# Output projection of the first ten token tiles, moved from its own stage into the last heads of attention

## The reference

```python
def _L0_attn_ref(x, w_qkv, w_out):
    ...
    scores = jnp.einsum('bihd,bjhd->bhij', q, k) * scale
    weights = jax.nn.softmax(scores, axis=-1)
    attn = jnp.einsum('bhij,bjhd->bhid', weights, v)
    concat = attn.transpose(0, 2, 1, 3).reshape(b, t, NUM_HEADS * DIM_HEAD)
    return jnp.einsum('btf,ef->bte', concat, w_out)
...
x = x + 0.5 * _L0_ffn_ref(_layernorm(x, axis=-1), ...)
x = x + _L0_attn_ref(_layernorm(x, axis=-1), L0_attn_w_qkv, L0_attn_w_out)
x = x + 0.5 * _L0_ffn_ref(_layernorm(x, axis=-1), ...)
```

## Time and profile before

| | |
|---|---|
| median of the runs | 4123.88 us |
| the profiled execution, its own time | 4123.62 us |
| its span, first to last instruction | 4121.8 us |
| PE busy | 4007.0 us (97%) |
| DVE busy | 3718.5 us (90%) |
| ACT busy | 2452.9 us (60%) |
| POOL busy | 1097.2 us (27%) |

### The profile page before, as it was taken

How to read it: one execution, slowest core, us unless ns; L and a number is a source line. 1 busy time by engine, 2 the same in 40 slices (tenths; PEclk the granted TensorE clock), 3 DMA queues, 4 the chain that set the end, 5 groups by cost and what they waited for, 6 DMA issues and landing times. The chain is left out here.

```text
span 4121.8 us, 108893 instructions
## 1 busy us (share of the span) xinstructions
PE 4007.0 (97%) x46275; PEld 2419.0 (59%) x46275; DVE 3718.5 (90%) x6367; ACT 2452.9 (60%) x2774; POOL 1097.2 (27%) x1156
## 2 busy tenths in 40 slices
PE   3999999999999999999999999999999999899999
PEld 2777765558864447884454444444444444677777
DVE  7999993689999999999999999999999996799998
ACT  1222225467777777777777777777777778122222
POOL 3888873300000000000000000000000000288886
PEclk8999999999999999999999999999999999999999
DMA  3000002311010110001001001001100100100000
GB/s 134 1 1 1 1 1 100 123 57 29 21 40 20 30 31 28 22 26 35 23 27 32 29 20 40 21 29 31 29 21 28 33 26 9 34 16 16 16 16 21
DMA packets 77710, 125.58 MB, mean 30 GB/s; under 512 B 27688, under 2 KB 56744, under 8 KB 75432
## 3 DMA queue, kind: packets, MB, share of 16 engines
q1 hardware_dynamic: 77224, 118.62, 9.8%
HBM read 72.55 MB, written 36.31 MB: 26 GB/s over the span
## 5 line engine op out<-in xcount | busy, mean ns | idle before, releaser
L1090 DVE TENSOR_REDUCE stats<-ps_b 128x1 f32<-128x512 f32 x4016 | 2486.5, 681 | 106.9 <-PE ps_b L1139 6.3
L1077 ACT ACTIVATE probs<-ps_s 128x1024 f32<-128x1024 f32 x2048 | 1983.8, 1021 | 648.6 <-PE ps_s L1173 648.6
L1139 PE MATMUL ps_b<-w_ffn 96*32 96x512 bf16 x10688 | 1122.5, 381 | 6.2 <-PEq L758 5.9
L1151 PE MATMUL ps_o<-probs,w_qkvT 128*32 128x512 f32 x8192 | 1097.2, 592 | 0.6 <-ACT probs L1077 0.6
L1173 PE MATMUL ps_s<-w_ffn 99*32 99x512 bf16 x10752 | 987.4, 380 | 0.5 <-ACT probs L1077 0.5
L639 PE MATMUL ps_gu_f<-w_ffn,zT_f 128*128 128x352 f32 x2048 | 638.7, 466 | 20.6 <-DVE h_f L514 15.9
L1173 PEld LDWEIGHTS ps_s<-w_ffn 99*32 99x32 bf16 x10752 | 392.0, 98 | 347.1 <-issue 188.4
L1139 PEld LDWEIGHTS ps_b<-w_ffn 96*32 96x32 bf16 x10688 | 379.1, 96 | 350.7 <-issue 174.2
L1139 PE MATMUL ps_b<-K,Q 96*32 96x512 bf16 x5376 | 568.7, 381 | 0.2
L1173 PE MATMUL ps_s<-Q,K 99*32 99x512 bf16 x5632 | 512.2, 381 | 2.2 <-ACT probs L1077 1.8
L639 PEld LDWEIGHTS ps_gu_f<-w_ffn,zT_f 128*128 128x128 f32 x2048 | 384.8, 193 | 217.5 <-issue 20.6
(11 more groups left out here) (150 smaller groups left out, 3460.4 us busy)
## 6 DMA issues: line engine op xcount, KB each, us to landing
w_ffn<-qk_parts_dram SPq DMA_DIRECT2D x84, 192.0 KB
w_ffn<-qk_parts_dram SPq DMA_DIRECT2D x84, 128.0 KB
x_res<-in_L_attn_x SPq DMA_DIRECT2D x4, 2048.0 KB, 19.5
qk_parts_dram<-first_group SPq DMA_DIRECT2D x32, 256.0 KB, 3.0
qk_parts_dram<-factor SPq DMA_DIRECT2D x32, 256.0 KB, 2.9
qk_parts_dram<-qk_parts SPq DMA_DIRECT2D x32, 256.0 KB, 2.8
factor<-denom_dram SPq DMA_DIRECT2D x64, 128.0 KB, 5.3
out<-x_res SPq DMA_DIRECT2D x16, 512.0 KB, 2.7
```

What stands on the lines that cost most here:

```text
L1077: nc.scalar.activation(probs[:, (2 * kt + half) % 4, :], ps_s[:, half, :], ACT.Exp, scale=float(DH) ** -0.5).then_inc(exped, 1)
L1090: nc.vector.tensor_reduce(mx[:, s, k // 4, bass.ds(k % 4, 1)], ps_b[:, bank, :], AX.X, ALU.max).then_inc(bank_free, 1)
L1139: last = nc.tensor.matmul(ps_b[j:j + STRIP, bank, :], Q[s][0:PAIRS, qt * P + j:qt * P + j + STRIP], K[s][0:PAIRS, kb * 512:(kb + 1) * 512] ...
L1151: last = nc.tensor.matmul(ps_o[32 * c:32 * c + 32, :], V[s][:, kt, :], probs[:, (2 * kt + c // 2) % 4, (c % 2) * 512:(c % 2 + 1) * 512], s ...
```

## The change

The first five groups of the output projection (ten tiles of batch 0, whose heads were finished long before) move into attention. `part_of` deals out their 20 products, one for each of the 20 key tiles without maxima: four at the end of head 62 and 16 in head 63. PE issues a product behind the first half's scores of its key tile and ahead of the second half's. The results go to the three banks `ps_b`; behind every fourth product DVE adds the group and takes its statistics. The loops of the last block start at group 5 on PE and DVE. Banks, waits and steps of the groups that stay keep their numbers. The norm's scratch moves from a tensor of its own to free columns of `y`.

```diff
@@ attend_phase, DVE
+                        at = merge.part_of(g, kt)
+                        if at and at[1] == merge.PARTS - 1:
+                            merge.add(dve, merge_bank(at[0]), at[0])
@@ attend_phase, PE
+                def merge_part(i, part):
+
+                    if i == 0 and part == 0:
+                        pe.wait_ge(bank_free, fills_before(NH - 1))
+                        pe.wait_ge(m.out_scaled, 4 * KD * (B - 1))
+                    if i >= RING and part == 0:
+                        pe.wait_ge(merge.x_done, i - RING + 1)
+                    last = merge.multiply(merge_bank(i), i, part)
+                    if part == merge.PARTS - 1:
+                        last.then_inc(merge.y_done, 1)
...
                             if c % 2:
                                 last.then_inc(scored, 1)
+                            at = merge.part_of(g, kt)
+                            if at and c == 1:
+                                merge_part(*at)
@@ Merge
+    EARLY = 5
+    PARTS = G * KD
+    SPARE = 4
...
+    def part_of(self, g, kt):
+
+        at = (g - (B * H - 2)) * KT + kt - (KT - self.SPARE)
+        return divmod(at, self.PARTS) if 0 <= at < self.EARLY * self.PARTS else None
...
-        for i in range(self.NG):
-            b = i // self.PER_BATCH
+        for i in range(self.EARLY, self.NG):
...
-        for i in range(self.NG):
-            dve.wait_ge(self.y_done, i + 1)
...
+        for i in range(self.EARLY, self.NG):
+            self.add(dve, self.bank(i), i)
```

More of the change, by code:

```diff
@@ L932, in _, with attend_phase @@
                 sp.wait_ge(m.neg_loaded, 16 * NEG_LOADS)
-def attend_phase(nc, m):
+def attend_phase(nc, m, merge):
     NH = B * H
@@ L980, in heads, with merge_bank @@
             tail()
+        def merge_bank(i):
+            return ps_b[:, i % RING, :].rearrange("p (t d) -> p t d", t=merge.G)
         FILLS_AHEAD = 0
@@ L1201, in __init__, with multiply, add @@
         self.y_done, self.x_done, self.w_loaded = (ctx.enter_context(nc.semaphore(n)) for n in ("y_done", "x2_done", "ffn_w_back"))
+    def part_of(self, g, kt):
+        at = (g - (B * H - 2)) * KT + kt - (KT - self.SPARE)
+        return divmod(at, self.PARTS) if 0 <= at < self.EARLY * self.PARTS else None
+    def multiply(self, bank, i, part):
+        b, (t, k) = i // self.PER_BATCH, divmod(part, KD)
+        tile = (i * self.G + t) % KT
+        return self.nc.tensor.matmul(bank[:, t, :], self.m.group(b * KD + k)[:, tile * P:(tile + 1) * P],
+                                     self.m.w_outT[:, k, :], start=(k == 0), stop=(k == KD - 1))
+    def add(self, dve, bank, i):
+        nc, m, G = self.nc, self.m, self.G
+        dve.wait_ge(self.y_done, i + 1)
+        tiles = m.x[:, i * G:(i + 1) * G, :]
+        nc.vector.tensor_tensor(tiles, bank, tiles, ALU.add).then_inc(self.x_done, 1)
+        dve.wait_ge(self.x_done, i + 1)
+        for t in range(G):
+            last = nc.vector.bn_stats(m.stats[:, i * G + t, :], m.x[:, i * G + t, :])
+        last.then_inc(self.norm.stats_in, 1)
     def take_banks(self, banks):
@@ L1238, in tensor @@
                 pe.wait_ge(self.x_done, i - len(self.banks) + 1)
[L1239 to L1243, removed]
+            for part in range(self.PARTS):
+                last = self.multiply(self.bank(i), i, part)
             last.then_inc(self.y_done, 1)
@@ L1323, in program @@
                 for n in ("o_kept", "out_moved", "denom_inverted", "denom_stored", "factor_loaded", "out_scaled"))
-            attend_phase(nc, m)
-        ffn_phase(nc, m, "f2", out, lead=Merge(nc, m, Norm(nc, m, ctx, "n3", sb("norm3", [P, 5 * NT])), ctx))
+            merge = Merge(nc, m, Norm(nc, m, ctx, "n3", m.y[:].rearrange("p c d -> p (c d)")[:, 5 * P:]), ctx)
+            attend_phase(nc, m, merge)
+        ffn_phase(nc, m, "f2", out, lead=merge)
 INS = ["L0_attn_x", "L0_attn_w_qkv", "L0_attn_w_out", "L0_ffn_w_gate", "L0_ffn_w_up", "L0_ffn_w_down"]
```

## The result

The changed kernel took 4128.9 us (median of 20 runs, 4125.66 to 4132.37) against 4123.92 for the kernel before (20 runs): a ratio of 1.0013, 95% interval 1.0007 to 1.0019, 5.0 us slower. Forecast were 4125.1 us, between 4118 and 4134, and "same" within 0.2%. One execution, the profiled one of e5_pairs, took 5288.56 us at a granted clock of 0.75 from start to end and is left out of every time here; all others had about 0.99. The profiled execution's span is 4127.4 us, 5.6 more than before. 1.6 us of that arose ahead of the edited place: ACT's exponentials of key tile 11 of head 62 start at 3467.02, before at 3465.45.

What follows compares the result with a forecast made beforehand. Bounds taken: a loop through PE and ACT in the last head, DVE in the output projection. +2.6 + 2.0 - 6.9 + 3.5 + 0 = +1.2 us on 4123.62, plus 0.26 to the median: 4125.1 us, 80% range 4118 to 4134.

Steps and rivals of the forecast that it cites:

- PE becomes the bound: Attention, last head: with the product a key tile holds 2.17 us of PE, more than 1.975; +2.6 us.
- Change of shape: Attention: forty changes between 32-column strips and 128 columns, two for each of twenty products; +2.0 us.
- x: Attention: extra time of one product for changing the array's shape, 0 to 0.54 us, taken as 0.1.
- the upper bound: Attention: x = 0.54 us, from PE's tail of 0.16 twice and an exposed load of 0.11 twice.
- rival 2: Attention: each shape change empties PE, x 0.45 to 0.54; 4132 to 4134 us, 4138 with cold start; chance 0.19.
- rival 1: The forecast: PE-bound last head, x up to 0.3, POOL's stall eats half the saving; 4118 to 4130.6 us; chance 0.65.
- DVE's five groups: Output projection: DVE loses 5 groups of 1.38 us from its chain; -6.9 us.
- POOL's order: Output projection: POOL still scales the last group, so DVE waits longer at L536 for the first tile; +3.5 us.
- Clock: Start of the feed-forward: gate products between 5.1 us gained and 4.4 lost, taken as 0, PE's idle time being similar.
- (3): Output projection: POOL's scaling ends earlier than reckoned, so its stall does not bind; -2.3, 4121.6 us; chance 0.07.
- (4): Attention gets no longer, the products running in PE's waits or beside the strips; 4120.5 us; chance 0.05.
- (5): Whole kernel faster: x = 0, no stall on POOL and a warm start together; -9.4, 4114.5 us; chance 0.04.

Runs made afterwards that it cites:

- e5_pairs: Changed kernel with two products together at every second key tile instead of one at each; 4127.12 us against 4124.11 for the kernel before.
- e1: Changed kernel with each of the 20 products issued as four strips of 32 columns; 4123.1 us against 4124.11 for the kernel before.
- e2: Changed kernel with three of the feed-forward's four first steps three groups later; 4125.08 us against 4124.11 for the kernel before.
- e3: Changed kernel with groups 0 to 4 left out altogether (no projection, residual or statistics for ten tiles); 4119.21 us against 4124.11 for the kernel before.
- e6: Changed kernel with four bf16 matmuls of 128 columns in each product's place, ten tiles wrong; 4129.79 us against 4125.8 for the kernel before.
- e5b: The kernel of e5_pairs run once more for a profile; 4126.86 us against 4124.77 for the kernel before.
- e4: Changed kernel with the edits of e1 and e2 together; 4121.09 us against 4125.8 for the kernel before.

## Why the prediction came out as it did

The time fell within the range and on "same"; the forecast of +1.2 us was 3.8 us short, and one term, 4.0 us too small, makes that.

- **PE becomes the bound, +2.6:** right. In strips, where nothing else is added, attention is 46.5 - 43.7 = 2.8 us longer.
- **Change of shape, x between 0 and 0.54, taken as 0.1, +2.0:** the mechanism was right and the size was off. Measured is 0.30 to 0.31, 6.0 us for 20 products, by the profile and by taking it away (e1) and halving it (e5). This is the term that was mis-sized. The row it leaned on to the low side, 17 transposes with 64 columns among those of 128, has no strips of 32 in it and could not price leaving them. The parts behind the upper bound were 0.16 twice and 0.11 twice. Measured: 0.10 to 0.11 twice, and 0.09 to 0.10 for the fp32 load; the strips' load on the way back lies within one of the 0.10 and adds no part of its own. The first product after the barrier had the load right to 0.01, and that 0.11 alone was already the 0.1 that was taken, with nothing left for the emptying.
- **The Trainium skill's rule** ("TensorEngine Tiling (Array Packing)", Key Properties: a change of tiling mode drains TensorE): the trace agrees. PE starts the next shape 0.10 us late on the way in and again on the way out, for bf16 as for fp32. So what rival 2 names, PE emptied at each change, did happen, at two thirds of its least price (0.30 against 0.45): each emptying cost 0.10 and not the 0.16 of tail, and one load was exposed and not two. x = 0.30 is the very edge of what rival 1 allows. Rival 2's upper end is +10.0 by its own terms, not +10.2; nothing hangs on that.
- **DVE's five groups, -6.9:** right, 7.1 in e2. **POOL's order gives +3.5 back:** right in place, 3.1 measured, so the stage saved 4.0 instead of 3.4. In e1 and e3 L499 to L536 takes 5.07 and 4.98 us, 3.4 more than before: there POOL's scaling begins 25.4 us behind the last copy, in the changed kernel 25.0. DVE's wait before L536 was 2.74 us and not the 4.2 forecast, since L508 took 1.07 longer and POOL began earlier.
- **Clock, 0:** right by luck. The two gate products together took 0.3 us less, by the first of them 1.5 less and the second 1.2 more. The reason given, that PE's idle time would be near to what it was, does not hold: behind 4.0 to 4.2 us of idle time the first gate product took 7.93 us before, 6.67 in e1, 7.52 in e3 and 6.66 in e6, behind 5.32 us 6.45 in the changed kernel and 7.89 in e5b. Each is one execution; what sets the length was not found.
- **Rivals 3, 4 and 5** are out: DVE waits 2.74 us before L536 (3), attention is 8.7 us longer and 2.8 even in strips (4), and neither x = 0 nor a full clock came (5).

With x = 0.30 the sum is 2.8 + 6.0 - 4.0 - 0.3 = +4.5, against 5.0 measured (2.9 to 7.8 by the interval).

## What to carry to other kernels

A matmul that fills an idle slot costs its streaming only as far as the slot goes, and on top what it takes to change the array's shape: 0.31 us for there and back here. Issuing it in the shape of its neighbours took 6.0 us of that away, two together 2.9. Where work is taken off the engine that sets the end, look at once at what stands in the next engine's queue: here 3.1 of 7.1 us were spent in front of POOL, and three moved numbers brought them back. With both repairs (e4) the move gains some 4 us of 4124, which its times just fail to tell from nothing.

## What was not expected

While POOL scaled the last heads, DVE's small L508 took 1.24 us in the changed kernel and 0.37, 0.28, 0.33, 1.07 and 0.47 in e1, e3, e4, e5b and e6, where it takes 0.17 otherwise. In all six it ends 0.04 to 0.07 us after one of POOL's four instructions ends. The rows of e1:

```profile
3539.00 4.95 POOL L155 TENSOR_TENSOR v_then_heads<-v_then_heads,factor 128x512 f32<-128x512 f32 x4 [24.33 <-DMA factor<-denom_dram]
```

```profile
3539.92 0.37 DVE L508 TENSOR_SCALAR z_scale_f<-z_amax_f 128x16 f32<-128x16 f32 x1
```

One POOL instruction takes 4.95 / 4 = 1.24 us, so the first ends at 3540.24, and L508 ends at 3540.29. In the changed kernel the second ends at 3544.50 + 2 x 1.235 = 3546.97, and L508, which began 0.04 after the first had ended, ends at 3547.02. L499, a TENSOR_REDUCE beside the same L155, kept its 0.40 us. The Trainium skill ("SBUF — State Buffer", Who interferes with whom) has DVE and GpSimd share one pair of ports, which one instruction holds to its end, and counts tensor_scalar among what may want it and tensor_reduce on trn2 not; these rows agree. No kernel was made to try it. It cost nothing in the changed kernel and in e1: from L499 to L536 it is 4.70 and 5.07 us, with DVE waiting for POOL's L565 in both. In e4, where POOL waits for DVE, that stretch is 1.78 us instead of 1.63.
